# An audio tower with routed experts on one core: finer own waits on VectorE, routing in fewer small operations, and epsilon folded into the norms' aggregation

## Time and profile before

| | us |
|---|---|
| median of 3 runs | 250.39 |
| lowest, highest | 248.43, 250.43 |
| span of the profiled execution, first to last instruction | 235.5 |
| what the median has beyond that span | 14.9 |
| DVE busy, PE busy, ACT busy, POOL busy | 158.7, 214.5, 137.8, 125.6 |

### The profile page before, as it was taken

The page is one execution under the profiler, slowest core; times in us unless marked ns, Lnnn a source line. Parts: engine busy times, 40 slices in busy tenths (PEclk is TensorE's granted clock), DMA queues, the critical chain, the costliest instruction groups (busy, mean ns, idle before and its releaser), DMA issues.

```text
span 235.5 us, 5477 instructions
## 1 busy us (share of the span) xinstructions
PE 214.5 (91%) x1587; PEld 171.8 (73%) x1587; DVE 158.7 (67%) x686; ACT 137.8 (59%) x311; POOL 125.6 (53%) x202
## 2 busy tenths in 40 slices
PE   6897899999999997998899978999899799899993
PEld 4674678669678855875757966968888699789872
DVE  0069699999989989999679594673254221244995
ACT  2223996999787989555775204894436456334250
POOL 7436566936621367788767780566436345552000
PEclk9999999999999999999999999999999999999998
DMA  5999999930010111113111114466767577722753
GB/s 117 226 234 271 315 403 406 400 138 4 0 33 3 34 33 33 46 38 88 36 39 46 45 41 99 147 205 224 242 231 239 199 248 245 241 93 68 220 177 92
DMA packets 27295, 35.33 MB, mean 150 GB/s; under 512 B 5387, under 2 KB 20036, under 8 KB 27267
## 3 DMA queue, kind: packets, MB, share of 16 engines
q1 hardware_dynamic: 23137, 30.79, 41.4%
q0 software_dynamic: 3680, 4.04, 6.4%
q10 hardware_dynamic: 450, 0.16, 0.4%
HBM read 10.61 MB, written 14.34 MB: 106 GB/s over the span
## 4 chain that ended last, share of the span: by engine, by line
PE 26%; DVE 23%; POOL 14%; issue 13%; SPq 12%; DMA 8%; ACT 2%; DVEq 0%; POOLq 0%; ACTq 0%
POOL xs L543 10%; SPq L433 4%; SPq L444 4%; DVE stat L689 4%; SPq L435 3%; DMA blk_x<-xs 3%; DMA ys<-yblk,blk_x 3%; PE PS L1098 3%; POOL rstd L519 3%; PE PS L981 3%; PE PS L1173 2%; PE PS L1196 2%; PE PS L1205 2%; DVE x_sb L923 2%; DVE acc L959 2%
## 5 line engine op out<-in xcount | busy, mean ns | idle before, releaser
L548 POOL DMA_INDIRECT ys<-yblk,blk_x x37 | 36.0, 973 | 36.3 <-DVE yblk L950 28.7
L543 POOL DMA_INDIRECT xs<-rows_x,pos_x x30 | 36.1, 1202 | 10.6 <-issue 9.2
L661 ACT ACTIVATE gd<-PS,bias 128x373 f32<-128x373 f32 x48 | 26.9, 572 | 21.8 <-PE PS L1173 18.2
L1173 PE MATMUL PS<-xt_sb,w_all 128*128 128x373 f32 x96 | 37.6, 485 | 1.3 <-ACT xt_sb L641 0.7
L1180 PEld LDWEIGHTS PS<-w_all,gd 128*125 128x125 f32 x288 | 33.6, 187 | 3.7 <-ACT gd L661 1.3
L1180 PE MATMUL PS<-w_all,gd 128*125 128x128 f32 x288 | 34.7, 273 | 0.8 <-ACT gd L661 0.8
L672 ACT ACTIVATE gb_t<-PS,blk_w 128x128 f32<-128x128 f32 x58 | 18.2, 366 | 23.8 <-PE PS L1205 12.6
L519 POOL TENSOR_TENSOR rstd<-ve,mhalf 125x3 f32<-125x3 f32 x32 | 27.7, 865 | 2.5
L950 DVE TENSOR_TENSOR yblk<-PS,blk_w 128x128 f32<-128x128 f32 x29 | 8.4, 289 | 28.1 <-PE PS L1205 27.9
L516 POOL TENSOR_TENSOR ve<-mv,eps 125x3 f32<-125x3 f32 x32 | 6.4, 201 | 31.9 <-DVE mv L693 31.6
L923 DVE SCALAR_TENSOR_TENSOR x_sb<-PS,comb,x_sb 125x128 f32<-125x128 f32 x72 | 20.7, 343 | 3.9 <-PE PS L1180 3.2
(11 more groups left out here) (200 smaller groups left out, 436.5 us busy)
## 6 DMA issues: line engine op xcount, KB each, us to landing
blk_w<-w_all SPq DMA_DIRECT2D x29, 321.0 KB, 2.7
xs<-blank SPq DMA_DIRECT2D x1, 8256.0 KB, 25.8
blk_x<-xs SPq DMA_DIRECT2D x37, 64.5 KB, 1.9
yg<-ys SPq DMA_DIRECT2D x5, 336.0 KB
xt_sb<-in_xt SPq DMA_DIRECT2D x4, 375.0 KB, 7.0
x_sb<-in_x SPq DMA_DIRECT2D x4, 336.0 KB
out<-x_sb SPq DMA_DIRECT2D x8, 168.0 KB
w_all<-in_we SPq DMA_DIRECT2D x1, 1024.0 KB
```

Source lines behind the costliest of these rows:

```text
L543: pool.indirect_dma_start(xs, bass.IndirectOffsetOnAxis(ap=pos_x[:, b // 2, s, i:i + 1], axis=0), rows_x[:, k, s, j, :], None).then_inc(s_ ...
L548: pool.indirect_dma_start(ys, bass.IndirectOffsetOnAxis(ap=blk_x[n % SLOTS][:, t, D:XW].bitcast(u32), axis=0), yblk[n % YBUF][:, t, :], No ...
L661: act.activation(gd[:, k % GD, c, 0:TP], of("D1", n)[:, 0:TP], ACT.Gelu, bias=bias128[:, 2 + k % E * HC + c:3 + k % E * HC + c]).then_inc( ...
L1173: pe.matmul(f[:, 0:TP], w_all[:, k % E, c * 128:(c + 1) * 128], x32[:, DENSE[k // E], 0:TP], start=True, stop=True).then_inc(S["D1"], 1)
```

## The change

The orders of all engines and the work on PE and ACT stay as they are.

1. `ln_stats`: every `bn_stats` counts up a semaphore `s_st`; the first `bn_aggr` waits for the second `bn_stats`, the third for the third. The wait at the end goes; in its place the next norm of the same kind waits, before its first `bn_stats`, for the aggregation one norm back. In `at`, the three additions count up `h2` one by one and the statistics wait for them singly.
2. Each group's statistics get a third triple (0, 0, 128 x 1e-5) beside the two that `bn_stats` writes, so `bn_aggr` (now 9 numbers in, not 6) gives variance + epsilon. POOL's addition L516 goes, 32 times. The triples are written once at the start by 8 more DVE memsets.
3. `mp`, `g3`, `fin`: `link` is replaced by waits on the instruction that is really needed, with others in between; in `g3` one product moves between the index searches.
4. Routing: `topi` is compared as an integer (the copy `topf`, L863, goes). The additions to `pref` one group after another become three doubling steps over all groups and one for the carry. An expert's base row is put into the first tally, so `row_of` (L888) goes; a maximum straight to integers replaces sum and copy (L894, L895). In `cnt` the sum `eb` (L940), which nothing reads, goes.
5. POOL's setup writes `twos`, `fours`, `tally` instead of `pref` and `eps`.

```diff
-            def ln_stats(i, n, src):
+            def ln_stats(i, n, src, made=None):
+                if n > 0:
+                    dve.wait_ge(s_ve[i], n)
                 for j in range(NJ):
-                    last = dve.bn_stats(stat[i][:, j, :], src[j])
-                link(last)
+                    if made and j != 1:
+                        wait(dve, made, NJ * n + (2, 2, 3)[j])
+                    dve.bn_stats(stat[i][:, j, 0:6], src[j]).then_inc(s_st[i], 1)
                 wait_nth(dve, normed[i], n - 2)
                 for j in range(NJ):
+                    if j != 1:
+                        dve.wait_ge(s_st[i], NJ * n + (2, 2, 3)[j])
                     last = dve.bn_aggr(mv[i][:, n % 2, j, :], stat[i][:, j, :])
                 last.then_inc(s_ve[i], 1)
-                dve.wait_ge(s_ve[i], n + 1)
...
+            for v in stat:
+                dve.memset(v[:, :, 6:8], 0.0).then_inc(S["pad"], 1)
+                dve.memset(v[:, :, 8:9], D * EPS).then_inc(S["pad"], 1)
...
                     pool.wait_ge(s_ve[i], n + 1)
-                    pool.tensor_tensor(ve[i][:, n % 2, :], mv[i][:, n % 2, :, 1], eps[:], ALU.add).then_inc(s_rstd[i], 1)
-                    pool.wait_ge(s_rstd[i], k + 1)
-                    pool.tensor_tensor(rstd[i][:, n % 2, :], ve[i][:, n % 2, :], mhalf[:], ALU.pow)\
+                    pool.tensor_tensor(rstd[i][:, n % 2, :], mv[i][:, n % 2, :, 1], mhalf[:], ALU.pow)\
...
-                    dve.tensor_tensor(m12[:], y[:, :, 1, :], y[:, :, 2, :], ALU.max)
-                    link(dve.tensor_tensor(m01[:, :, 0:P - 1], y[:, :, 0, 1:P], y[:, :, 1, 1:P], ALU.max))
+                    wait(dve, "ht", n)
+                    dve.tensor_tensor(m12[:], y[:, :, 1, :], y[:, :, 2, :], ALU.max).then_inc(S["mx"], 1)
+                    dve.tensor_tensor(m01[:, :, 0:P - 1], y[:, :, 0, 1:P], y[:, :, 1, 1:P], ALU.max).then_inc(S["mx"], 1)
+                    wait(dve, "mx", 2 * n + 1)
...
+                    wait(dve, "mx", 2 * n + 2)
...
-                    wait(dve, "ht", n + 1)
...
-                    link(last)
-                    link(dve.reciprocal(grec[:], gsum[:]))
-                    link(dve.tensor_tensor(dd[:], top[:, :, 1], top[:, :, 0], ALU.subtract))
-                    dve.tensor_tensor(dd[:], dd[:], grec[:], ALU.mult).then_inc(S["dd"], 1)
...
-                    link(dve.tensor_copy(topf[:], topi[:, :, 0:2]))
...
-                        last = dve.tensor_tensor(to, pref[:, n, i, :], m[:, i, :], ALU.add)
-                        if k + 1 < len(own):
-                            link(last)
+                    link(dve.tensor_tensor(twos[:, PAD:, :], t[:, PAD:, :], t[:, PAD - 1:PAD + NI, :], ALU.add))
+                    link(dve.tensor_tensor(fours[:, PAD:, :], twos[:, PAD:, :], twos[:, PAD - 2:PAD + NI - 1, :], ALU.add))
+                    dve.tensor_tensor(pref[:, si, :, :], fours[:, PAD:PAD + NI, :], fours[:, 0:NI, :], ALU.add)\
+                        .then_inc(S["mask"], 1)
+                    dve.tensor_tensor(tally[:, si + 1, PAD, :], fours[:, PAD + NI, :], fours[:, NI, :], ALU.add)\
+                        .then_inc(S["car"], 1)
...
-                    link(dve.tensor_reduce(pos[:, n, :, :], row_hot[:], AX.X, ALU.add))
-                    dve.tensor_copy(pos_x[:, n, :, :], pos[:, n, :, :]).then_inc(S["pos"], 1)
+                    dve.tensor_reduce(pos_x[:, n, :, :], row_hot[:], AX.X, ALU.max).then_inc(S["pos"], 1)
...
-                    link(dve.tensor_reduce(eb[:], passed[:], AX.X, ALU.add))
...
-                    link(last)
+                        last.then_inc(S["acc"], 1)
                     for j in range(NJ):
+                        if j != 1:
+                            wait(dve, "acc", NJ * n + (2, 2, 3)[j])
```

More of the change, by code:

```diff
@@ L38 @@
 ITEMS = {q: [i for i in range(NI) if 2 * q + i % 2 in SPARSE] for q in SPAIRS}
+PAD = 4
 GD = 3
@@ L129 @@
 """
+INIT = 21
 def runs(ns):
@@ L293, in audio_tower @@
         be2_sb = sb("be2_sb", [E, D])
-        stat = [sb(f"stat{i}", [P, NJ, 6]) for i in range(4)]
+        stat = [sb(f"stat{i}", [P, NJ, 9]) for i in range(4)]
         mv = [sb(f"mv{i}", [P, 2, NJ, 2]) for i in range(4)]
-        ve = [sb(f"ve{i}", [P, 2, NJ]) for i in range(4)]
         rstd = [sb(f"rstd{i}", [P, 2, NJ]) for i in range(4)]
@@ L323, in audio_tower @@
         s_rstd = [sem(f"s_rstd{i}") for i in range(4)]
+        s_st = [sem(f"s_st{i}") for i in range(4)]
         s_blank = sem("s_blank_out")
@@ L347, in normed_by @@
         def normed_by(i, n):
-            return sum(4 if (f"l{i + 1}", m) in ON_ACT else 2 for m in range(n))
+            return sum(3 if (f"l{i + 1}", m) in ON_ACT else 1 for m in range(n))
         def wait_so(eng, n):
@@ L794, in _ @@
                     wait(dve, "hr", n + 1)
-                    wait(dve, "h2", n - 1)
+                    wait(dve, "h2", NJ * (n - 1))
                     dve.tensor_copy(h[:, n % 2, :], of("hr", n)[0:P, 0:NJ * D]).then_inc(S[nth("h", n)[0]], 1)
@@ L837, in _ @@
                                                         flat(h[:, n % 2, :])[j], ALU.mult, ALU.add)
-                    last.then_inc(S["h2"], 1)
-                    wait(dve, "h2", n + 1)
-                    ln_stats(3, n, flat(h2[:, n, :]))
+                        last.then_inc(S["h2"], 1)
+                    ln_stats(3, n, flat(h2[:, n, :]), "h2")
                 if name == "g2":
@@ L871, in _ @@
                     si = SPAIRS.index(n)
-                    wait(dve, "rk", si - 1)
-                    m = mask[:, si % 2, :, :]
-                    link(dve.tensor_tensor(m, one[:, n, 0, :, :], one[:, n, 1, :, :], ALU.add))
-                    own = ITEMS[n]
-                    after = pref[:, n, NI, :] if n == SPAIRS[-1] else pref[:, SPAIRS[si + 1], ITEMS[SPAIRS[si + 1]][0], :]
-                    for k, i in enumerate(own):
-                        to = pref[:, n, own[k + 1], :] if k + 1 < len(own) else after
-                        last = dve.tensor_tensor(to, pref[:, n, i, :], m[:, i, :], ALU.add)
-                        if k + 1 < len(own):
-                            link(last)
-                    last.then_inc(S["mask"], 1)
+                    own = slice(ITEMS[n][0], ITEMS[n][-1] + 1, 1 if len(ITEMS[n]) == NI else 2)
+                    t, m = tally[:, si, :, :], tally[:, si, PAD + 1:PAD + 1 + NI, :]
+                    wait(dve, "rk_of", si)
+                    link(dve.tensor_tensor(m[:, own, :], one[:, n, 0, own, :], one[:, n, 1, own, :], ALU.add))
+                    link(dve.tensor_tensor(twos[:, PAD:, :], t[:, PAD:, :], t[:, PAD - 1:PAD + NI, :], ALU.add))
[4 more added lines that the diff above has]
+                        .then_inc(S["car"], 1)
                 if name == "rk":
@@ L1144, in _ @@
                     v = f[0:P, 0:NI * E]
-                    pe.matmul(v, before[:], mask[:, si % 2, :, :].rearrange("p i e -> p (i e)"), start=True, stop=False)
-                    pe.matmul(v, ones[:], pref[:, n, 0:NI, :].rearrange("p i e -> p (i e)"), start=False, stop=True)\
+                    pe.matmul(v, before[:], tally[:, si, PAD + 1:PAD + 1 + NI, :].rearrange("p i e -> p (i e)"),
+                              start=True, stop=False)
+                    pe.matmul(v, ones[:], pref[:, si, :, :].rearrange("p i e -> p (i e)"), start=False, stop=True)\
                         .then_inc(S["rk"], 1)
                 if name == "cnt":
-                    wait(pe, "mask", SPAIRS[-1] + 1)
+                    wait(pe, "car", len(SPAIRS))
                     f = claim(name, n, ("full", n + 1))
-                    pe.matmul(f[0:P, 0:E], ones[:], pref[:, SPAIRS[-1], NI, :], start=True, stop=True).then_inc(S["cnt"], 1)
+                    pe.matmul(f[0:P, 0:E], ones[:], tally[:, len(SPAIRS), PAD, :], start=True, stop=True).then_inc(S["cnt"], 1)
                 if name == "ct":
```

73 lines of the change are left out of this document (39 added, 34 removed).

## The result

| | before | changed | ratio, 95% interval |
|---|---|---|---|
| first comparison: median (lowest to highest) | 250.41 (248.43 to 250.95) | 240.61 (237.85 to 241.81) | 0.9585 (0.9509 to 0.966) |
| second, with more runs | 239.62 (236.32 to 242.22) | 233.2 (230.55 to 236.54) | 0.976 (0.9658 to 0.9861) |
| third | 240.23 (236.91 to 243.87) | 233.53 (232.09 to 235.64) | 0.9755 (0.9681 to 0.9829) |
| fourth | 241.16 (237.38 to 243.84) | 233.47 (232.17 to 235.87) | 0.9811 (0.9765 to 0.9857) |

All in us, all executions counted in the medians, the undisturbed ones alone in the ratios. 240.61 lies just under the range of 240.8 to 247.6. The prediction was a ratio of 243.9 / 250.39 = 0.974; the three later comparisons, all on one chip, on which the kernel before takes 240 us and not 250, are at 0.976, 0.9755 and 0.9811.

What follows compares the result with a forecast made beforehand. No single engine bounds it: DVE paces 31.9 to 86 us with PE 91% full, then POOL's scatters, then PE in the blocks. 1.1 + 2.6 + 0.3 + 2.0 + 0.5 = 6.5 us off 250.39 gives 243.9; range 240.8 to 247.6.

Steps and rivals of the forecast that it cites:

- The price of an own wait: On DVE: waiting on the instruction just issued costs 0.13 us, regained if the finer wait replacing it is already met.
- Own waits cost nothing: Rival: only removed instructions count, on POOL and before `scat.18`; 3.0 us less, 247.4; chance 0.05.
- the slower rival: Rival: the new waits stop DVE's overlap as the old ones did, norm about 1.1 us or more; 252.9; chance 0.04.
- Step 1: Single chain up to 31.9 us: savings in norms and POOL's additions, together 1.1 us.
- Steps 2 and 3: 31.9 to 86 us: 2.6 gained, over half of PE's 4.5 spare; then `p3.5` before `scat.0`: 0.3.
- The first rival: PE becomes the bound in the middle stretch: 0.5 there, 1.5 among scatters; 3.9 us less, 246.5; chance 0.18.
- The sign named for it: PE's first 35 to 86 us holding as many matmuls as before would show that PE becomes the bound.
- Step 4: POOL's scatters: four L516 fewer 1.1, the 1.39 us wait down to 0.30, `p4.6` 0.3; of 2.5, 2.0 taken.
- Step 5: The 37 blocks start from the last scatter and keep their length: 0, with PE as full as it is.
- Step 6: The end: `fin` gives 0.65, but PE's last matmul and a `da` limit it; 0.5 us taken.
- the 14.9 us around it are taken as they are: Whole kernel: savings were reckoned against the profiled span of 235.5 us and taken from the median of 250.39.
- the third rival: The blocks give some back because their transfers fall differently: 4.5 us less, 246 and a bit; chance 0.06.

## Why the prediction was wrong by a little

By its own steps, the sizes counted from the undisturbed profiles.

- **The price of an own wait** (0.13 us) and the norm at 0.80: right, 0.82. "Own waits cost nothing" is out: item 1, which takes no instruction away, is worth 2.46 us at `scat.0`. So is the slower rival: the finer waits, met, did not stop the overlap.
- **Step 1**, the first stretch, 1.1: right, 1.10 between the first and the 21st aggregation and 0.12 in the first norm, and the split (0.26 + 0.26 for the waits, 0.54 for POOL) near enough (0.58 and 0.43 by the parts alone).
- **Steps 2 and 3**, 2.6 + 0.3 to `scat.0`: 2.36. The way it was reckoned, from the slack of PE and not from the 6.8 us that DVE loses, held: DVE lost some 5.9 us and 3.5 of it came back as waits. "Somewhat over half of PE's spare time" was a little too kind. The first rival, that PE becomes the bound, foresaw these waits for PE and is wrong about the size here (0.5). The sign named for it, as many matmuls of PE in 35 to 86 us as before, came true (335 and 337 against 333), but it was badly chosen: between equal marks PE does the same 370 in 52.95 us instead of 55.30.
- **Step 4**, 2.0 among the scatters: 0.47. This is the term that failed most, in two of its parts. The four additions L516 were to give 1.1 and gave 0.45: 0.31 at `p3.7`, but only 0.14 in front of `scat.10`, because there POOL, which waited for nothing before, now waits 0.66 us for DVE's statistics of `p4.5`. The wait in front of `scat.18` was to give another 1.1 and gave 0.06. The step sized `rk.2` by what DVE's gate saves in front of it (0.9 + 0.45 + 0.45) and took PE as a matter of busy share. It is a matter of place: `rk.2` stands behind `D1.10 sc1.6 D1.11`, and PE reached it 4.2 us earlier than before (115.31 against 119.54), no more than `scat.10` had already gained (102.56 against 107.10). The saving of the gate vanished in the 2.2 us between `pref` and `rk.2`. With `rk.2` moved (and no filler) the scatters were 1.19 us shorter at once.
- **Step 5**, the blocks keep their length: right in the profiles (92.04 against 92.36 and 92.13). How long they took in the executions of 250 us, from whose median the forecast started, no profile shows.
- **Step 6**, 0.5 at the end: from the first `fin` to the end 16.51 became 16.28 in both later profiles, 0.23. From `T.0` to the end nothing of it is left.

So the steps give 1.10 + 2.36 + 0.12 + 0.47 + 0.27 = 4.3 us in the traces where 6.5 were forecast, and the medians of three comparisons give more than the traces: 6.4, 6.7 and 7.7 us, or 4.6 to 5.9 by the ratios (1 - 0.9811 and 1 - 0.9755, of 241). Some of this is half clock, which an execution meets or not; that the kernel before meets it more often was not shown.

Why 240.61 then lay under the range: the step that failed is the one before the sum, "the 14.9 us around it are taken as they are". There are 1.7 to 3.7 us around a span in all later runs. By that the other 11 to 13 of the 250.39 were inside the execution, in something that the profile shown had not met. Late starts and half clock are what other profiles show; no execution of 250 us was profiled, so what it was stays open. The forecast let all of it stand unchanged. Between the two medians of the first comparison 9.8 - 4.3 = 5.5 us went that the steps do not account for. A range around a sum from an undisturbed profile was too narrow for a time that was disturbed by 5%. One small slip besides: the third rival's 4.5 us less is 245.9, not "246 and a bit".

## What to carry to other kernels

Set the profiled span against the time: when they differ by more than the few microseconds around a span, the profile is of another kind of execution than the time, and the forecast needs a term for what it does not show. Cutting some 5.9 us of an engine's own time bought 2.4 us, and the rest became waits for others; in a fixed order a saving ends at the next piece that stands in front of its user, and so look for the piece, not for the busy share. When parts of a change are tried alone, compare lengths between marks in the trace: they repeated to 0.03 us where the times of one kernel differed by 1.1%.

## What the runs showed of the hardware

- Nine numbers in a `bn_aggr` took 164 ns where six took 160. And a finer own wait that is already met costs nothing that can be seen: `bn_stats`, `bn_aggr` and the next norm still overlap by 0.09 us each. The Trainium skill's page "VectorE: DVE Perf Modes", section "The DRAIN you can't avoid", says that the next operation does not start until the pipe is empty, and adds that one that is not held starts earlier. The overlap agrees with that addition, which the prediction left out. The section also says of eight copies that a semaphore after each costs nothing extra; that does not carry over to the own waits here, with which a norm took 1.06 us and with the finer ones 0.82.
- PE falls from 2.4 to 1.2 GHz for about 3.4 us (0.50 in one window of 2 us, 0.65 in the next) in some executions and not in others of the same kernel, each time after idle time: in the 2 us just before the fall it had been busy for 0.38 to 1.01 us, in all fourteen such falls between 20 and 220 us in these profiles. One such stretch costs 1.6 us where PE's results are waited for. At 182 us, in the stream, nothing can be seen of it: `T.0` to the end took 92.36 and 92.13 with it, and 92.35 (no filler) and 92.32 (all but item 1) in two variants without it.
- The start varies by itself: the first aggregation stood between 12.60 and 14.92 us in the changed kernels and between 13.73 and 14.86 in the one before. In the profile before, 24 matmuls of the small convolution (64*64, 64x192) took 2.20 us; in the changed kernel's first profile 1.21. The latest first aggregation, 14.92, is that of an execution with half clock from 8.7 to 12.1 us.
